# A head's two output products moved from the third quarter to behind the next head's query projection

## The reference, cut to what matters

```python
q_c = hidden_size @ Wq_c.T + bq_c                      # 192 wide
q = (q_c @ Wq_up.T + bq_up).reshape(b, s, NH, Q_HEAD)  # 32 heads of 192
kv = hidden_size @ Wkv_c.T + bkv_c                     # 64 latent + 64 rope
...
scores = jnp.einsum('bhqd,bhkd->bhqk', q, k) / np.sqrt(Q_HEAD)
attn = jax.nn.softmax(scores, axis=-1)
o = jnp.einsum('bhqk,bhkv->bhqv', attn, v)
out = jnp.einsum('bhsv,Hv->bsH', o, Wo) + bo
```

## Time and profile before

| | |
|---|---|
| runs of the kernel before | 1948.34, 1952.21, 1953.28 us |
| the profiled execution | 1951.58 us |
| its span | 1949.9 us |
| mean granted TensorE clock | 0.991 of full speed |
| busy, share of the span | PE 97%, DVE 83%, ACT 73%, POOL 64% |
| attention | from about 100 to about 1831 us |

### The profile page before, as it was taken

How to read it: one execution, slowest core, us unless ns; L and a number is a source line. 1 busy time by engine, 2 the same in 40 slices (tenths; PEclk the granted TensorE clock), 3 DMA queues, 4 the chain that set the end, 5 groups by cost and what they waited for, 6 DMA issues and landing times. The chain is left out here.

```text
span 1949.9 us, 37654 instructions
## 1 busy us (share of the span) xinstructions
PE 1897.3 (97%) x11020; PEld 1202.1 (62%) x11020; DVE 1608.9 (83%) x2601; ACT 1424.8 (73%) x2525; POOL 1238.7 (64%) x1347
## 2 busy tenths in 40 slices
PE   6989999999999999999999999999999999999799
PEld 5746666666666666666666666666566666666476
DVE  6678888888888888888888888888888888888665
ACT  4667777777777777777777777777677777777443
POOL 3347767767767767766767767767676676676700
PEclk9999999999999999999999999999999999999899
DMA  5421111111111111111111111111111111111211
GB/s 200 170 82 43 32 43 43 33 43 43 35 43 43 33 43 43 33 43 43 33 44 43 32 43 43 32 43 44 33 35 41 43 37 38 43 39 29 76 43 43
DMA packets 74310, 95.21 MB, mean 49 GB/s; under 512 B 25856, under 2 KB 48416, under 8 KB 74272
## 3 DMA queue, kind: packets, MB, share of 16 engines
q1 hardware_dynamic: 70176, 86.33, 16.5%
q0 software_dynamic: 4096, 8.40, 1.2%
HBM read 83.95 MB, written 10.75 MB: 49 GB/s over the span
## 5 line engine op out<-in xcount | busy, mean ns | idle before, releaser
L946 DVE TENSOR_TENSOR PTL<-X,PTH 128x512 f16<-128x512 f32 x1024 | 657.6, 684 | 128.0 <-ACT PTH L895 127.5
L895 ACT ACTIVATE PTH<-X 128x512 f16<-128x512 f32 x1024 | 554.2, 594 | 231.4 <-PE X L804 231.4
L963 DVE TENSOR_REDUCE mx<-S 128x1 f32<-128x1024 f32 x512 | 622.0, 1215 | 5.4 <-PE S L824 5.4
L911 ACT ACTIVATE prob<-S,shift,unscale 128x1024 f32<-128x1024 f32 x512 | 620.0, 1211 | 6.3 <-DVE shift L969 6.3
L804 PE MATMUL X<-ident,prob 128*128 128x128 f32 x4096 | 541.3, 275 | 11.5 <-ACT prob L911 11.5
L804 PEld LDWEIGHTS X<-ident,prob 128*128 128x128 f32 x4096 | 459.5, 141 | 139.3 <-ACT prob L911 57.7
L822 PE MATMUL S<-kvTH,qeH 128*128 128x512 f16 x1024 | 389.1, 380 | 3.1 <-POOL qeL L731 3.1
L823 PE MATMUL S<-kvTL,qeH 128*128 128x512 f16 x1024 | 389.1, 380 | 0.0
L824 PE MATMUL S<-kvTH,qeL 128*128 128x512 f16 x1024 | 389.1, 380 | 0.0
L766 POOL TENSOR_TENSOR onormH<-osum,recip_row 128x512 fp32r<-128x512 f32 x128 | 197.1, 1540 | 273.6 <-ACT osum L920 273.6
L829 PE MATMUL O<-PTH,kvn 128*128 128x512 f16 x1024 | 263.5, 380 | 0.0
(11 more groups left out here) (237 smaller groups left out, 2093.6 us busy)
## 6 DMA issues: line engine op xcount, KB each, us to landing
recip_row<-row_scratch SPq DMA_DIRECT2D x128, 256.0 KB, 4.1
weff<-weff_scratch SPq DMA_DIRECT2D x128, 192.0 KB, 3.9
wv<-in_wv POOLq DMA_DIRECT2D x128, 64.0 KB, 2.6
raw<-in_raw SPq DMA_DIRECT2D x8, 772.0 KB, 7.1
weff_scratch<-w_split SPq DMA_DIRECT2D x8, 768.0 KB, 5.6
x<-in_x SPq DMA_DIRECT2D x4, 1024.0 KB, 6.9
x_all<-in_x SPq DMA_DIRECT2D x3, 1024.0 KB, 6.2
out<-y SPq DMA_DIRECT2D x3, 1024.0 KB, 4.2
```

The costliest lines, as they stand in the source:

```text
L895: nc.scalar.activation(PTH[p][:, part:part + 4, unit * P:(unit + 1) * P], X[:, k % 2, :].rearrange("p (k c) -> p k c", k=4), ACT.Copy).the ...
L911: nc.scalar.activation(prob[u][:], S[:, u % 2, :], ACT.Exp, bias=shift[:, col:col + 1], scale=keep["unscale"][:, 0:1], accum_out=rs[:, col ...
L946: v.tensor_tensor(PTL[p][at], X[:, k % 2, :].rearrange("p (k c) -> p k c", k=4), PTH[p][at], ALU.subtract).then_inc(low_out, 1)
L963: v.reduce_max(mx[:, col:col + 1], S[:, u % 2, :], AX.X).then_inc(max_ready, 1)
```

## The change

The two output products of a head leave the third quarter (u == 2) of step g, where they served head g-2. They now stand in the first quarter (u == 0), behind the query projection, and serve head g-3. So they are issued one step later by number. What hangs on this follows: the bias product that starts a block's sum stands at h = 2 instead of h = 1, the last product of a block stops the sum at h = 2, VectorE's copy of V stands in u == 2 of h == 2, the steps 0 to 3 of a block are unrolled instead of 0 and 1 and the loop begins at pair 2, and TensorE and VectorE have three steps behind the last block instead of two. No instruction of a head is added or removed, and no transfer is moved. The `wait_ge` for `onorm_high` is dropped (that for `onorm_low` comes later in GpSimd's order). GpSimd's code is as before, and its wait for `wv_done`, g-2, now asks for products that stand in step g instead of step g-1.

```diff
-                for h in (0, 1):
-                    body(b * NH + h, b, h, h)
-                with eng.Fori(1, NH // 2 - 1) as pair:
+                for h in range(4):
+                    body(b * NH + h, b, h, h % 2)
+                with eng.Fori(2, NH // 2 - 1) as pair:
...
-                on, one, two = exists(g), exists(g - 1), exists(g - 2)
+                on, one, three = exists(g), exists(g - 1), exists(g - 3)
...
                     if u == 0 and on and exists(g + 1):
                         next_queries()
+                    if u == 0 and three:
+                        pe.wait_ge(wv_split, g - 2)
+                        pe.wait_ge(onorm_low, g - 2)
+                        mm(V[:], wvH[1 - par][:], onormH[:], start=False, stop=False)
+                        mm(V[:], wvHL[1 - par][:], onormLH[:], start=False, stop=isinstance(h, int) and h == 2).then_inc(wv_done, 1)
...
-                    if u == 2 and two:
-
-                        pe.wait_ge(wv_split, g - 1)
-                        pe.wait_ge(onorm_high, 2 * g - 2)
-                        pe.wait_ge(onorm_low, g - 1)
-                        mm(V[:], wvH[par][:], onormH[:], start=False, stop=False)
-                        mm(V[:], wvHL[par][:], onormLH[:], start=False, stop=isinstance(h, int) and h == 1).then_inc(wv_done, 1)
...
-                if isinstance(h, int) and h == 1 and on:
+                if isinstance(h, int) and h == 2 and on:
...
-            steps(pe, body)
+            steps(pe, body, after=3)
...
-                    if u == 3 and isinstance(h, int) and h == 1 and b:
+                    if u == 2 and isinstance(h, int) and h == 2 and b:
...
-            steps(dve, body)
+            steps(dve, body, after=3)
```

## The result

The changed kernel takes 2020.57 us (median of 4 runs, 2017.66 to 2022.77), the kernel before in the same comparison 1951.66. The ratio is 1.0365, with a 95% interval of 1.0351 to 1.0378: 3.65% slower. The forecast of 2116 had the direction and the mechanism, but a loss of 164 us where there are 69; 2020.6 is within 3 us of what the prediction gave for its case (A), 2018. The time lies inside the stated range, since that reached down to (A); as a forecast of the size it was wrong.

A forecast was written before the change was run, and what follows sets the result against it. TensorE looked binding (97% busy), but GpSimd's phase would make VectorE's shift wait. Over 125 heads, 1.33 us each gives 166, less 2 saved: 164 on 1951.6, forecast 2116 us, range 1995 to 2132.

The forecast's parts named there:

- (A): Second-quarter shift gets through when GpSimd's L773 ends: period 13.84 us, 0.58 more a head, 2018 us; chance 0.32.
- TensorE's two products in their place: Between query projection and first-quarter transposes: same 0.47 us, no wait; those transposes start at 0.47.
- Q1: First pass over u: the 0.08 us stall before the value products goes; the next pass's transposes start at 3.73.
- Q2 is bound by ScalarE at 3.02, so the place alone costs 0.12 a head, 15 us: Second pass over u: ScalarE's copies and exp need 3.02 us, so only 0.27 of the removed 0.47 comes back.
- (C): Rival: GpSimd doesn't hold the shift at these pairs; 15 us lost, less 8 for the additions: 1958 us, chance 0.07.
- GpSimd starts 0.87 after 0: After the query projection's issue in each head, wvH starts 0.87 us later, putting L767 at 4.22 to 5.76.
- The shift of Q1 at 4.58 ends at 5.78, X of Q3 at 7.16: First-quarter shift on VectorE is held until GpSimd's L767 ends; third-quarter transposes start at 7.16, 0.4 us later than without this.
- (B): Second-quarter shift waits past L773 until L731 ends: period 14.59 us, 1.33 more a head, 2116 us; chance 0.45.
- The additions of block 3: 6 us saved in (A): GpSimd's block-3 additions would block the third-quarter shift for less; with block 2's smaller step, about 6 us saved.

The follow-up runs named there:

- the lock taken away: Changed kernel with the shift as a tensor_scalar having mx as its only tensor input: 1958.5 us, 1.0049 of the kernel before.
- The probes: Kernel before with rows of unread GpSimd instructions behind L731 at four single steps, in two single runs of differing rows: 1970.01 us and 1957.68 us.
- the run with one copy: Changed kernel with one more unread 128 x 128 scaled copy on GpSimd ahead of the onorm chain: 2000.58 us, ratio 1.0269.

## Why the prediction was right in its mechanism and wrong in its size

- *TensorE's two products in their place*: 0.47 us, X of Q1 at 0.47. Right.
- *Q1*: the stall before the value products would go and X of Q2 stand at 3.73. It is at 3.71. Right.
- *Q2 is bound by ScalarE at 3.02, so the place alone costs 0.12 a head, 15 us.* Right in kind: with the lock taken away Q2 takes 3.04. The period is 13.42 there, 0.16 over the kernel before: Q3 takes 3.30 as well, the 0.05 that the prediction had put into (A) alone. 1958.5 us remain where (C) had said 1958 (7 to 10 us over the kernel before, since the additions' stall went too).
- *GpSimd starts 0.87 after 0.* It starts at 0.86, and L767 runs from 4.21 to 5.73 (forecast 4.22 to 5.76).
- *The shift of Q1 at 4.58 ends at 5.78, X of Q3 at 7.16.* It ends at 5.75, X is at 7.21; the transposes follow the exp 1.43 after its start, where I had taken 1.35. Right.
- **The step that failed: "I take (B)"**, that the shift of Q2, met by L773, is passed over by L731 behind it and costs 0.75 us more at the head of Q0. It was let in 0.02 us after L773 in each of the 121 heads in which it met it, and X of Q0 stands at 10.50 (case (A): 10.46). 0.75 x 125 = 94 us of the forecast's 164 were this step. I took the row with the same instruction and the like lengths, 5.36 us in the earlier trace rows, as nearest. The row that spoke against it, L751 and L752 with no pause between the earlier trace rows, was the better guide, and so is the unpaused pair of L766 and L767, which only the later runs showed. The trace of the kernel before had more on this side that I overlooked: in 11 heads the same shift started 0.43 to 0.46 us before the end of the same L731 as in the row of 5.36 and was let in 0.02 after it, with GpSimd's next entry (10 times the start of a transfer) following at once. The probes show that the 5.36 us are no property of feed-forward code, and that there is no simple rule: I should have held (A) and (B) as equal and not let one rare row price 125 heads. Why the row of 5.36 went the other way stays open.
- *The additions of block 3: 6 us saved in (A).* Wrong too. There the shift of Q3 was held for 5.11 us, over three additions and two of GpSimd's copies behind them, and the head takes 19.95 where the kernel before took 20.37. With the conversion of block 2, which costs nothing now, some 2.5 us were saved.
- That 2020.6 lies within 3 us of (A)'s 2018 is in part luck: the head grew by 0.62 instead of 0.58 (5 us more over 125) and the additions gave some 3 us less, while the heads at the block ends grew less than the others (by 0.53, from 13.16 to 13.69) and the start of the attention lost nothing.

The Trainium skill's rule ("SBUF — State Buffer", "Who interferes with whom": the loser is blocked for the whole instruction) had given (A), and in the regular heads the trace agrees: every wait ends 0.02 us after one GpSimd instruction. With rows of instructions without a wait it doesn't hold as a bound: 2.77, 3.86 and 5.07 us in the probes, over two, three and four instructions of the row.

## What to carry to other kernels

A tiny instruction on the critical chain can be the one that pays for a change elsewhere: before moving work, ask which engine's phase hangs on it, and compare where in time that engine's instructions will then stand with where the short two-input VectorE instructions of the other chain stand. Where a VectorE instruction reads two tensors from SBUF beside a busy GpSimd, try the form that takes the [P, 1] operands as scalars; here that was worth 8 us to the old kernel, 62 to the changed one. And when a timeline shows work that is "hidden" only by its phase, more or less of it can go either way: 0, 0.41 and 0.82 us of additional GpSimd work gave 2020.6, 2000.6 and 1965.4 us.

## What was not expected of the hardware

In the run with one copy, a shift that started 0.27 to 0.29 us before the recorded end of L768 ended 0.02 after that end (18 heads), one that started 0.09 to 0.18 before it had no delay at all (65 heads, 0.22 us), and one that started 0.08 to 0.11 before it was held for the whole of the next instruction (40 heads, 1.57 to 1.60 us). The limit isn't the same everywhere: ahead of the probes' rows shifts that started 0.15 to 0.25 before qeL's recorded end were held too. A tensor_scalar with two per-partition scalars from SBUF was never held: 512 instructions with a mean of 0.27 us beside the same GpSimd work that held the two-tensor form. A waiting VectorE instruction can be passed over several times by a row of GpSimd instructions with no wait between them, and in the one place where it was tried a wait of GpSimd for its own result (a pause of 0.17 us behind qeL) ended that: 0.47 instead of 5.36 us.
